# D times x added by GpSimd inside the scan, attention's sums inverted in quarters among later experts, gate with another norm order and GpSimd's output bias

## What is computed

```python
# layer 1, "attention": a scan, here over 2 sequences of 2048 tokens
z, x_ssm, Bm, Cm, dt = split(layernorm(x) @ in_proj_w.T)
y = selective_scan(x_multi, A, Bm, Cm, dt)         # h = clip(dA*h + x B, -10, 10); y = C h
y = y + x_multi * Dparam[None, None, :, None]      # "D times x"
y = y * silu(z)
y = layernorm(y); y = clip(y @ out_proj_w.T, -10, 10)
s = layernorm(y)
# layer 1, feed-forward
h = gelu(xn @ w1[sel] + b1[sel]); reasoned = h @ w2[sel] + b2[sel]
f = xn + 0.3 * (reasoned @ Wo + bo)
x = x + s * silu(f)
# attention of layer 0: softmax's denominators are sums that are inverted once for all rows
```

## Time and profile before

| | us |
|---|---|
| three runs | 1969.68, 1975.33, 1976.43 |
| median | 1975.33 |
| the profiled execution | 1973.51 |
| its span, first to last instruction | 1971.7 |

### The profile page before, as it was taken

How to read it: one execution, slowest core, us unless ns; L and a number is a source line. 1 busy time by engine, 2 the same in 40 slices (tenths; PEclk the granted TensorE clock), 3 DMA queues, 4 the chain that set the end, 5 groups by cost and what they waited for, 6 DMA issues and landing times.

```text
span 1971.7 us, 41333 instructions
## 1 busy us (share of the span) xinstructions
PE 1765.1 (90%) x15442; PEld 680.1 (34%) x15442; DVE 1644.6 (83%) x2545; ACT 1519.8 (77%) x2881; POOL 462.2 (23%) x755
## 2 busy tenths in 40 slices
PE   7799999999999999999999999989954668799884
PEld 4322222222222222222222222258722234366552
DVE  7799999999999999999999999634435547588688
ACT  6479999999999999999999999953314448777454
POOL 2332300320002322322322220000074553000024
PEclk9899999999999999999999999999967779899796
DMA  3413212211111111111111120148642333422221
GB/s 116 160 66 102 66 62 66 74 38 28 33 37 40 49 50 41 49 50 41 50 48 41 50 64 13 38 127 229 193 120 75 88 105 91 125 71 80 91 70 32
DMA packets 155710, 146.36 MB, mean 74 GB/s; under 512 B 39242, under 2 KB 134477, under 8 KB 155362
## 3 DMA queue, kind: packets, MB, share of 16 engines
q1 hardware_dynamic: 147170, 126.56, 21.8%
q0 software_dynamic: 8352, 17.29, 3.0%
HBM read 80.80 MB, written 60.03 MB: 71 GB/s over the span
## 4 chain that ended last, share of the span: by engine, by line
PE 71%; ACT 11%; DVE 6%; another core or an unknown queue 5%; issue 3%; DMA 2%; SPq 1%; POOL 1%; DVEq 0%; ACTq 0%; POOLq 0%
PE PS L1869 27%; PE PS L1897 16%; PE PS L1853 10%; ACT probs L1256 6%; PE PS L1947 3%; PE PS L2142 2%; PE PS L1932 2%; PE PS L2124 1%; PE PS L2214 1%; DVE YM L906 1%; PE PS L2145 1%; PE PS L2059 1%; PE PS L2127 1%; PE PS L1924 1%
## 5 line engine op out<-in xcount | busy, mean ns | idle before, releaser
L818 DVE TENSOR_REDUCE mxp<-PS 128x1 f32<-128x1024 f32 x1024 | 1171.4, 1215 | 24.8 <-PE PS L1853 18.8
L1256 ACT ACTIVATE probs<-PS 128x512 f32<-128x512 f32 x2048 | 1094.8, 597 | 62.0 <-PE PS L1897 17.9
L1869 PE MATMUL PS<-probs,VH 128*32 128x256 f32 x8192 | 641.8, 391 | 1.9 <-ACT probs L1256 0.6
L1897 PE MATMUL PS<-stacks 51*128 51x512 bf16 x2048 | 439.0, 387 | 19.5 <-ACT probs L1256 16.6
L1853 PE MATMUL PS<-stacks 48*128 48x512 bf16 x2048 | 417.3, 379 | 9.8 <-DMA stacks<-qkl_d 8.6
L1869 PEld LDWEIGHTS PS<-probs,VH 128*32 128x32 f32 x8192 | 173.0, 108 | 413.3 <-issue 230.3
L1897 PEld LDWEIGHTS PS<-stacks 51*128 51x128 bf16 x2048 | 116.2, 93 | 458.6 <-ACT probs L1256 415.9
L1723 POOL DMA_INDIRECT VP<-oe_d,ROWI x128 | 131.2, 1025 | 258.8 <-DMA oe_d<-stacks 164.9
L1615 POOL DMA_INDIRECT xe_d<-xn_s,rows_s x128 | 126.4, 987 | 216.2 <-PE PS L1869 173.3
L1593 POOL CAST spl<-nmx 128x8 bf16<-128x8 f32 x64 | 12.1, 189 | 504.9 <-DVE nmx L813 295.9
L1853 PEld LDWEIGHTS PS<-stacks 48*128 48x128 bf16 x2048 | 105.7, 95 | 25.5 <-DVE mxp L818 13.4
(11 more groups left out here) (361 smaller groups left out, 1850.3 us busy)
## 6 DMA issues: line engine op xcount, KB each, us to landing
stacks<-qkl_d SPq DMA_DIRECT2D x128, 96.0 KB
xe_d<-zt SPq DMA_DIRECT2D x16, 640.0 KB
stacks<-xe_d SPq DMA_DIRECT2D x32, 320.0 KB, 3.8
oe_d<-stacks SPq DMA_DIRECT2D x32, 320.0 KB, 3.3
stacks<-qkl_d SPq DMA_DIRECT2D x128, 64.0 KB
o_d<-SG SPq DMA_DIRECT2D x256, 32.0 KB
ews<-in_ew_dram SPq DMA_DIRECT2D x33, 192.0 KB, 2.4
probs<-xs_d SPq DMA_DIRECT2D x18, 256.0 KB, 4.0
```

The costliest lines, as they stand in the source:

```text
L818: v.tensor_reduce(mxp[:, n // 2, n % 2:n % 2 + 1], MXB[n % 2].rearrange("p a c -> p (a c)"), X_AX, ALU.max).then_inc(mx_done, 1)
L1256: act.activation(probs[:, at:at + 512], PS[:, bank_of(u, e), :], ACT.Exp, scale=float(1.0 / np.sqrt(np.float32(DK)))).then_inc(exp_done, 1)
L1869: mm = pe.matmul(OB[32 * jg:32 * jg + 32, c:c + 256], VH[w][:, kt, :], probs[:, at:at + 256], start=(kt < 2 and half == 0), stop=(kt >= TC ...
L1897: pe.matmul(PS[:, bank_of(u, e), :], KS[w][o:o + KROWS + 3, kt * P:(kt + 1) * P], QS[w][o:o + KROWS + 3, q0:q0 + 512], start=True, stop=Tr ...
```

## The change

1. **Experts.** The loads of the sums move behind `refill_tokens(4)` and `(5)`, two of them in each of SP's steps e = 0 to 7. DVE adds and inverts a quarter of the columns behind each of experts 10 to 13, and `sum_weights` comes behind expert 14. SP's stores to `rl_d` move from step 8 to step 16.
2. **Scan.** POOL does two `tensor_tensor` of 128 x 512 per chunk: D·x into `XD` when the chunk is loaded, and `YS` += `XD` after `y_out`. SP's `load_chunk(c)`, c ≥ 4, also waits for POOL's sum of chunk c − 4.
3. **Gate.** `gated` no longer has the four `scalar_tensor_tensor`; x isn't loaded (16 loads instead of 32), and all four groups have a room of their own. The bias goes off PE: a one-row matmul before the scan and DVE's `tensor_scalar` make `bo3` = 0.3·bo, and POOL adds it to `XN2` in 8 `tensor_tensor` of 128 x 512 behind its work of the scan; `gate_in` waits for them. `normed` moves from step `s == GROUPS1 + 1` to the step before, ahead of `finish_pair`.

A branch that is only taken when a bound on the state is passed (not in the profiled execution) is changed to match; it is left out here.

```diff
@@ rooms
-        XG = [[kept[2 * i] for i in range(GP)], [probs[:, 2 * i * 512:(2 * i + 1) * 512] for i in range(GP)]]
-        ZG = [[kept[2 * i + 1] for i in range(GP)], [probs[:, (2 * i + 1) * 512:(2 * i + 2) * 512] for i in range(GP)]]
+        XD = [kept[0], kept[2]]
+        ZG = [[kept[2 * i + 1] for i in range(GP)], [probs[:, (2 * i + 1) * 512:(2 * i + 2) * 512] for i in range(GP)],
+              [probs[:, 2 * i * 512:(2 * i + 1) * 512] for i in range(GP)], [kept[2 * i] for i in range(GP)]]
@@ SP
-            for half in range(2):
-                hold(oe_st[half], 64 * UNITS)
-            for j in range(NB):
+            def load_sums(j):
                 for odd in range(2):
                     sp.dma_start(LS[odd][G * j:G * j + G, :], o_d[odd, :, DK, j * 512:(j + 1) * 512]).then_inc(at_ld[0], 16)
@@ load_chunk
                 hold(c_done, c - 3)
+                if c >= 4:
+                    hold(xd_done, XD_BASE + c - 3)
@@
             refill_tokens(4)
             refill_tokens(5)
+            for half in range(2):
+                hold(oe_st[half], 64 * UNITS)
             for e in range(E):
                 refill_tokens(e + 6)
                 if e + 4 < E:
                     hold(mo_ready, e + 1)
                     load_weights(sp, e + 4)
-                if e == 8:
+                if e < NB:
+                    load_sums(e)
+                if e == 2 * NB:
                     hold(at_sum, 1)
@@ load_pair
-                sp.dma_start(XG[s % 2][i].rearrange("p (t c) -> p t c", t=2), xg[:, 2 * k:2 * k + 2, :]).then_inc(xz_ld[i], 16)
-                sp.dma_start(ZG[s % 2][i].rearrange("p (t c) -> p t c", t=2), zg[:, 2 * k:2 * k + 2, :]).then_inc(xz_ld[i], 16)
+                sp.dma_start(ZG[s][i].rearrange("p (t c) -> p t c", t=2), zg[:, 2 * k:2 * k + 2, :]).then_inc(xz_ld[i], 16)
@@
+            hold(xd_done, XD_BASE + TCH)
             load_pair(0, GP - 1)
             for s in range(1, GROUPS1):
                 for i in range(GP):
-                    hold(xz_ld[i], 32 * s + 16)
-                    if s >= 2:
-                        hold(yT_ready, NB + GP * (s - 2) + i + 1)
-                        hold(var_ready, LN9 + VAR[("a", s - 2)])
+                    hold(xz_ld[i], 16 * s + 16)
                     load_pair(s, i)
@@ DVE
+            def sums_inverse(quarter):
+                c = slice(P * quarter, P * (quarter + 1))
+                v.wait_ge(at_ld[0], 32 * NB)
+                link(v.tensor_tensor(LS[0][:, c], LS[0][:, c], LS[1][:, c], ALU.add))
+                ins = v.reciprocal(LS[0][:, c], LS[0][:, c])
+                if quarter == 3:
+                    ins.then_inc(at_sum, 1)
+
             def sum_weights():
-                v.wait_ge(at_ld[0], 32 * NB)
-                link(v.tensor_tensor(LS[0], LS[0], LS[1], ALU.add))
-                v.reciprocal(LS[0], LS[0]).then_inc(at_sum, 1)
                 v.wait_ge(rows_done, 1)
@@
-                if e == 3:
+                if 0 <= e - NB - 2 < 4:
+                    sums_inverse(e - NB - 2)
+                if e == NB + 6:
                     sum_weights()
@@
             v.wait_ge(l1_ready, 3)
+            v.tensor_scalar(bo3[:, :], PS[:, 6, P:P + D], 0.3, None, ALU.mult)
@@ gated
-                v.wait_ge(xz_ld[i], 32 * (s + 1) + 16)
-                x4 = XG[s % 2][i].rearrange("p (t h n) -> p t h n", t=2, h=NH1)
-                y4 = YS[:, 2 * k:2 * k + 2, :].rearrange("p t (h n) -> p t h n", h=NH1)
-                for h in range(NH1):
-                    ins = v.scalar_tensor_tensor(x4[:, :, h, :], x4[:, :, h, :], sc_aff[:, 0, h * HP:h * HP + 1], y4[:, :, h, :], ALU.mult, ALU.add)
-                link(ins)
-                link(v.tensor_tensor(XG[s % 2][i], XG[s % 2][i], ZG[s % 2][i], ALU.mult))
+                v.wait_ge(xz_ld[i], 16 * (s + 1) + 16)
+                v.wait_ge(xd_done, XD_BASE + 2 * k % TCH + 2)
+                link(v.tensor_tensor(ZG[s][i], ZG[s][i], YS[:, 2 * k:2 * k + 2, :].rearrange("p t n -> p (t n)"), ALU.mult))
@@ gate_in
                 v.wait_ge(fo_ready, j + 1)
+                v.wait_ge(xd_made, XM_BASE + TCH + j + 1)
@@
                 elif s == GROUPS1:
                     gate_in(2 * s - 1)
-                elif s > GROUPS1:
                     normed(GROUPS1 - 1)
@@ ACT, ahead of the gate
+            act.wait_ge(xd_made, XM_BASE + TCH)
             act.wait_ge(fw_ld, 16 * B)
@@ POOL
+            for c in range(TCH):
+                xd, w = XD[c % 2], c % 4
+                pool.wait_ge(tile_ld[w], TILE_BASE + 96 * (c // 4 + 1))
+                after(pool, xd_done, XD_BASE + c - 1 if c >= 2 else 0)
+                pool.tensor_tensor(xd.rearrange("p (b n) -> p b n", b=B), XS[w].rearrange("p (b n) -> p b n", b=B),
+                                   sc_aff[:, 0, :].unsqueeze(1).broadcast_to([P, B, DI]), ALU.mult).then_inc(xd_made, 1)
+                pool.wait_ge(xd_made, XM_BASE + c + 1)
+                pool.wait_ge(y_out, c + 1)
+                yc = YS.rearrange("p (b c) n -> p b c n", b=B)[:, :, c, :]
+                pool.tensor_tensor(yc, yc, xd.rearrange("p (b n) -> p b n", b=B), ALU.add).then_inc(xd_done, 1)
+            pool.wait_ge(xnT_out, 2 * NB)
+            for j in range(NB):
+                xn = XN2[:, TB * j:TB * (j + 1), :]
+                pool.tensor_tensor(xn, xn, bo3[:, :].unsqueeze(1).broadcast_to([P, TB, D]), ALU.add).then_inc(xd_made, 1)
@@ PE, before the scan and in routed_out
-            pe.matmul(PS[:, 6, 0:B], ones1[:, :], s1_[:, 1, :], start=True, stop=True).then_inc(l1_ready, 1)
+            pe.matmul(PS[:, 6, P:P + D], ones1[:, :], r1[:, E1:E1 + D], start=True, stop=False)
+            pe.matmul(PS[:, 6, 0:B], ones1[:, :], s1_[:, 1, :], start=False, stop=True).then_inc(l1_ready, 1)
@@
-                pe.matmul(tiles4(PS[:, 7, :]), ones1[:, :], each(r1[:, E1:E1 + D]), start=True, stop=False)
                 for t in range(TB):
-                    mm = pe.matmul(PS[:, 7, t * P:(t + 1) * P], RT[m % 2][:, t, :], wo1[:, :], start=False, stop=(t == TB - 1))
+                    mm = pe.matmul(PS[:, 7, t * P:(t + 1) * P], RT[m % 2][:, t, :], wo1[:, :], start=(t == 0), stop=(t == TB - 1))
```

25 lines of the change are left out of this document (21 added, 4 removed).

## The result

The kernel after takes 1960.96 us in the median of 4 runs (1959.04 to 1963.71), the kernel before beside it 1975.88 (4 runs). The ratio is 0.9928, with a 95% interval of 0.9906 to 0.9949: some 14 us faster. The forecast was 1955.5 us, with a range of 1944 to 1968: direction and range hold, the gain was put 4 us too high.

The account below looks back on a forecast made before the run. It took PE as the bound in nearly all of the span, with DVE leading in the gate. Experts −6.0, scan +5 and gate −17 made −18: 1973.5 − 18 = 1955.5 us, range 1944 to 1968.

Parts of the forecast that it names:

- Experts: Expert stage: tokens asked for before the sums and the reciprocal in quarters remove PE's losses, −6.0 us, bounds −4.5 and −6.5.
- the three stalls: Experts' transposes: PE loses 3.13 us waiting for tokens, 1.65 at its lower clock, 1.20 behind the reciprocal.
- Scan: Scan stage: POOL's added instructions hold up DVE instructions with two SBUF inputs, +5 us, bounds 0 and +25.
- I take one, because a late DVE also delays its L1008: Scan chunks: DVE loses one POOL instruction per chunk, usually only at L1023; period 8.39 us, +4.6 over 15 periods.
- the rival with both hit: Scan chunks: both POOL instructions hit DVE in each chunk, period 9.72 us, scan +25, total 1975.5 us; chance 0.13.
- 0.4 at most: Before the scan: the one-row matmul and the tensor_scalar for the bias add 0.4 us at most.
- Gate: Gate stage: without 64 L1088 on DVE and the one-row matmuls on PE, −17 us, bounds −24 and −8.
- Group 0: Gate's first group: DVE's gain of 4.5 us pays for hits by POOL's bias additions; 0 taken for both.
- Groups 2 and 3: Gate groups bound by DVE: 5.6 us net each, 11.2 for both, plus 2.4 from PE keeping its clock.
- The one-row matmuls: Gate groups 0 and 1, bound by PE and ACT: three matmuls of 1.15 us lie in the path, 3.4 us gained.
- The norm's place: End of the gate: `normed` ahead of the pair before last changes who waits, by 1 us either way.
- PE and ACT binding early: Gate rival: PE's work and ACT's table loads stand in line, gain only 8 us, total 1964.5 us; chance 0.15.

Follow-up runs that it names:

- e8_bias_in_scan: e2_moved with the bias's eight additions on POOL moved into the scan's first eight chunks, started by the end of L1030; 1946.77 us, ratio 0.9869.
- e1_narrow: Kernel after with POOL's 32 scan instructions narrowed from 512 to 8 columns, waits and order kept; 1950.15 us, ratio 0.9863.
- e2_moved: Kernel after with POOL's full scan work at other times, product and sum started beside DVE instructions with an input in PSUM; 1950.90 us, ratio 0.9875.
- e4_bias_pe: Kernel after with the bias back in PE's one-row matmul and POOL's eight additions gone; 1958.51 us, ratio 0.9919.
- e5_no_dx: Kernel before without its 64 L1088 in the gate (D times x left out), x still loaded; 1956.12 us, ratio 0.9910.
- e12_halves: e8_bias_in_scan with the norm in its old place and the bias added in halves of 256 columns, one per chunk; 1944.60 us, ratio 0.9832.
- e7_norm: Kernel after with the norm back in the last step, behind the closing of the pair before; 1959.01 us, ratio 0.9937.

## Why the prediction was right, and where it was not

**Experts: right.** −5.96 against −6.0, each of the three stalls gone, and alone they bring 7.9 us (3.0 to 12.6). The quarter took 0.95 and not 0.84 us, which hid as well. SP's stores of the inverse cost nothing at their new place.

**Scan: right mechanism, a term of the sum too small, and one left out.** "I take one, because a late DVE also delays its L1008" was right for two chunks of three. The step that failed is to take this state as steady, with a period of 7.06 + 1.33 = 8.39. A hit costs 1.06 us, not the whole POOL instruction, since POOL's has begun by then, and DVE's own work is 6.94 us and not 7.06 (e8_bias_in_scan); so the chunk, 8.01 us, fits into PE's 8.09, DVE catches up, and the third chunk is the rival's, with both hit. The mean is the same by accident: 14 periods cost 3.83 us, 0.27 each, where 0.31 was taken. In the rival with both hit I added whole instructions (9.72); the double hit costs 2.13 and a chunk 9.0.

What was missing is the edges. In the last chunk PE has no sums (L2124, L2127) of a next one to do while DVE makes the state: it waited 3.56 us for L1043 instead of 2.04, so the hits of 0.46 and 1.06 us on L1038 and L1041 before it (1840.00 and 1841.06) came through whole, 1.52 us. L1072 behind the scan was hit by POOL's bias, 0.69. And the copy at the start took 1.97 us instead of 0.17. With "0.4 at most" before the scan I weighed only the matmul and the `tensor_scalar`, and not POOL's first product, which meets DVE when PE has nothing else to do: 1.80 us of delay and 1.11 of PE's low clock behind it, less the 0.75 that the kernel before had lost to the clock, 2.17 in this pair of traces. Together 3.83 + 1.52 + 0.69 + 2.17 = +8.2 against +5. e1_narrow and e2_moved show that the first two go away with the collisions; for the third, e4_bias_pe has no bias on POOL and 12.80 us behind the scan (e2_moved has 12.83 with the bias there, since its L1072, 0.31 us, meets POOL at another moment).

**Gate: the total right, its parts not.** −16.8 in the profiled pair against −17. By stretch it is −3.2, −2.7, −4.4, −7.1 and +0.6. Group 0 was put at 0: "bound by PE and ACT", and 4.5 us of DVE's gain paid back to the bias. The first half of this was wrong: in the kernel before PE waited 1.20 and 1.44 us for L1092 there. Alone, the gain is 5.0 (e5_no_dx), and the bias pays back 1.3 (e2_moved against e12_halves) to 3.0 us of it (after against e12_halves; part of the 3.0 is PE's low clock). So the zero was wrong by some 3 us. Groups 2 and 3 were put at 5.6 each plus 2.4 for the clock, 13.6: they gave 11.5. That the sum of the parts comes to 17 again is luck: too little in groups 0 and 1 (5.9 against 3.4), too much in groups 2 and 3. Collisions of L1113 in them were there as forecast (0.97 and 1.60 us in group 3), and PE's clock didn't stay high throughout (L2241 of group 1 took 5.46 us, 3.84 in e7_norm). The one-row matmuls were put at 3.4; with L1088 gone they are worth 2.5, one in each of groups 1 and 2 and 0.1 in group 3. The norm's place cost 0.7, inside the 1 us; it was counted as 0. Of the rivals, PE and ACT binding early (gain 8) falls: L1088 alone was worth 18 us (12.8 to 22.9).

**The whole.** −6.0 + 8.2 − 16.8 + 0.8 (untouched stages) = −13.8 in the span. The forecast of −18 missed by the scan's 3.2 us and by what the untouched stages did.

## What to carry to other kernels

Work given to POOL is free only beside DVE instructions that don't want the same port: write down DVE's instructions with their inputs, find the stretches with an input in PSUM or with no work, and start POOL by a semaphore at the head of such a stretch, not when its data happen to be ready. If a piece is longer than the stretch, cut it. And when an added delay feeds back into who comes first, don't take one state for the steady one: ask whether the loop stays there, and look at the first and the last pass for themselves.
